# A copy of each tile's rows on GpSimd between the load and its readers, in a mixture-of-experts stage

## What is computed

```python
x = x + tanh(g_xattn[0]) * attention(layernorm(x), ctx, ctx, ...)      # 16 batches x 256 tokens x 256, 16 heads
x = x + tanh(g_ffn[0]) * ffn(layernorm(x), ...)
# ffn, E = 8 experts, K = 2 of them for each token:
bids = sigmoid(x @ conf_w.T + conf_b) * wealth
top_bids, selected = top_k(bids, 2)
combine = sum(one_hot(selected, 8) * softmax(top_bids)[..., None], axis=2)
expert_out[e] = (silu(x @ gate_w[e].T) * (x @ up_w[e].T)) @ down_w[e].T          # 256 -> 1024 -> 256
output = einsum('ebsh,bse->bsh', expert_out, combine)
```

## Time and profile before

| | |
|---|---|
| median of 3 runs | 1151.61 us (1150.68 to 1152.59) |
| the profiled execution | 1148.98 us |
| its span | 1147.2 us |
| TensorE busy | 1069.5 us, 93% |
| VectorE, ScalarE, GpSimd busy | 56%, 48%, 30% |
| mean granted TensorE clock | 0.971 |
| loads of `xg` | 39 of 272 KB |

### The profile page before, as it was taken

One profiled execution on the slowest core, in us unless ns is written; L12 is line 12 of the kernel. 1 busy time (PEld: TensorE's weight loads), 2 busy tenths in 40 slices (PEclk: granted clock), 3 DMA queues, 4 the chain that ended last, 5 costly groups with the idle time before them and its releaser, 6 DMA issues. The chain is left out here.

```text
span 1147.2 us, 24335 instructions
## 1 busy us (share of the span) xinstructions
PE 1069.5 (93%) x8310; PEld 892.5 (78%) x8310; DVE 647.4 (56%) x1575; ACT 547.4 (48%) x877; POOL 347.4 (30%) x404
## 2 busy tenths in 40 slices
PE   5789999999999978898999999999899999999994
PEld 4556767777777755575999999999579999999993
DVE  3657777777777764447444444444754444444442
ACT  4466777777777744445333333333643333333331
POOL 2024545554545552513112112112311211211211
PEclk8799999999999989999999999999999999999997
DMA  7000111111111173466212112112461211211211
GB/s 240 25 21 20 50 39 43 63 38 38 47 38 38 49 272 146 141 240 225 58 23 38 33 23 38 33 23 38 160 234 19 38 33 23 38 33 23 38 33 16
DMA packets 48426, 79.41 MB, mean 69 GB/s; under 512 B 6400, under 2 KB 42240, under 8 KB 44544
## 3 DMA queue, kind: packets, MB, share of 16 engines
q0 software_dynamic: 18080, 50.93, 16.5%
q1 hardware_dynamic: 30304, 27.95, 8.3%
HBM read 53.42 MB, written 25.18 MB: 69 GB/s over the span
## 5 line engine op out<-in xcount | busy, mean ns | idle before, releaser
L1809 POOL DMA_INDIRECT out<-y,token x64 | 103.7, 1620 | 473.3 <-DVE y L1693 352.7
L1585 ACT ACTIVATE silu<-gate 128x512 f32<-128x512 f32 x128 | 76.8, 600 | 277.0 <-PE up L1424 277.0
L960 DVE TENSOR_REDUCE max_neg<-maxps 128x4 f32<-128x1024 f32 x128 | 156.5, 1223 | 56.1 <-PE maxps L547 56.0
L1436 PE MATMUL down<-w_split,h_hi 128*128 128x512 f32 x512 | 185.8, 398 | 0.0
L1684 DVE TENSOR_TENSOR h<-silu,up 128x512 f32<-128x512 f32 x128 | 88.1, 688 | 171.0 <-ACT silu L1585 171.0
L1424 PE MATMUL gate<-x_hi,w_split 128*128 128x256 f32 x1024 | 184.1, 281 | 0.0
L1424 PE MATMUL up<-x_hi,w_split 128*128 128x256 f32 x1024 | 184.0, 281 | 0.0
L759 ACT ACTIVATE probs<-scores 128x1024 f32<-128x1024 f32 x124 | 127.3, 1026 | 86.4 <-PE scores L572 85.2
L1424 PEld LDWEIGHTS gate<-x_hi,w_split 128*128 128x128 f32 x1024 | 148.8, 188 | 2.9
L1424 PEld LDWEIGHTS up<-x_hi,w_split 128*128 128x128 f32 x1024 | 147.8, 188 | 0.0
L1438 PE MATMUL down<-w_split,h_lo 128*128 128x256 f32 x512 | 144.0, 281 | 0.0
(11 more groups left out here) (203 smaller groups left out, 1762.5 us busy)
## 6 DMA issues: line engine op xcount, KB each, us to landing
xg<-dispatched SPq DMA_DIRECT2D x39, 272.0 KB, 2.8
stage<-gate_T POOLq DMA_DIRECT2D x10, 1024.0 KB, 7.2
stage<-up_T POOLq DMA_DIRECT2D x10, 1024.0 KB, 9.4
stage<-down_T POOLq DMA_DIRECT2D x10, 1024.0 KB, 11.5
ctxT<-ctxT SPq DMA_DIRECT2D x17, 256.0 KB, 2.9
x_all<-x SPq DMA_DIRECT2D x16, 256.0 KB, 5.1
out<-x_all SPq DMA_DIRECT2D x16, 256.0 KB, 2.1
out<-y,token POOLq DMA_INDIRECT x70, 3.8
```

What stands on the lines that cost most here:

```text
L960: V.tensor_reduce(to, maxps[:], AX.X, ALU.max, negate=True).then_inc(s["max_taken"], 1)
L1436: mm(down[t][:].rearrange("p (n d) -> p n d", n=2), h_hi[:, i, rows], split[:, :, cols], start=i == 0, stop=False, skip_group_check=True)
L1585: nc.scalar.activation(silu[pair % 2][:], gate[pair % 2][:], ACT.Silu).then_inc(s_silu, 1)
L1809: pool.indirect_dma_start(out, bass.IndirectOffsetOnAxis(token[:, t:t + 1], axis=0), y[:, t, :], None, compute_op=ALU.add).then_inc(s_adde ...
```

## The change

A second buffer `rows` of the same shape as `xg`. GpSimd copies each landed tile from `xg` to `rows` (`copy_rows`), counted by the new semaphore `s_copied`. TensorE's transposes and VectorE's notes read `rows`. The load of the next tile waits for the copy and no longer for the notes. The copy of tile n+2 stands on GpSimd in body n, behind the (first) scatter, and waits until tile n+1 has been transposed and noted. VectorE's notes of tile n+1 move from the start of body n+1 into `next_rows` of body n, and take all eight weights of a row instead of one. Two unused loads run at the end instead of one. The two early tiles are still read from `xg`.

```diff
-        noted_weight = sb("noted_weight", [P, TT])
+        noted_weights = sb("noted_weights", [P, TT, EXPERTS])
+        rows = sb("rows", [P, TT, ROW])
...
             def first(e, r, n):
-                sp.wait_ge(s_noted, n)
+                if e == EARLY:
+                    sp.wait_ge(s_noted, EARLY)
+                else:
+                    sp.wait_ge(s_copied, n + (1 - EARLY) - 1)
...
             def rest(e, j, r, n):
-                sp.wait_ge(s_noted, n)
+                sp.wait_ge(s_copied, n + (1 - EARLY) - 1)
                 load_rows(j * TILE + (e * REGION + FIRST))
...
-            sp.wait_ge(s_noted, done + EXPERTS)
-            load_rows(0)
+            for more in range(2):
+                sp.wait_ge(s_copied, done + (EXPERTS + more - EARLY))
+                load_rows(0)
...
+            def turn_rows(copies):
+
+                pe.wait_ge(s_copied, copies)
+                turn(rows, 1)
...
-                turn_rows(n * 16 + 32)
+                turn_rows(n)
...
-            def note_rows(e):
-                V.tensor_copy(noted_token[:], xg[:, :, TOKCOL].bitcast(i32))
-                V.tensor_copy(noted_weight[:], xg[:, :, COMB + e]).then_inc(s_noted, 1)
-
-            def next_rows(r, n, firsts):
+            def note_rows():
+                V.tensor_copy(noted_token[:], rows[:, :, TOKCOL].bitcast(i32))
+                V.tensor_copy(noted_weights[:], rows[:, :, COMB:COMB + EXPERTS]).then_inc(s_noted, 1)
+
+            def next_rows(e, r, n, firsts):
...
                 V.tensor_copy(token[:], noted_token[:])
-                V.tensor_copy(weight[:], noted_weight[:]).then_inc(s_moved, 1)
+                V.tensor_copy(weight[:], noted_weights[:, :, e]).then_inc(s_moved, 1)
                 dve.wait_ge(s_moved, n + (1 - EARLY))
+                note_rows()
                 dve.wait_ge(s_down, n + 1)
...
+            def copy_rows(tile):
+
+                alone.wait_ge(s_rows, tile * 16 + 16)
+                if isinstance(tile, int) and tile == EARLY:
+                    pool.wait_ge(s_noted, EARLY)
+                else:
+                    pool.wait_ge(s_turned, tile)
+                    pool.wait_ge(s_noted, tile)
+                nc.gpsimd.tensor_copy(rows[:], xg[:]).then_inc(s_copied, 1)
...
             add_early(0, s_added)
             pool.wait_ge(s_added, 16)
+            copy_rows(EARLY)
             add_early(1, s_first_added)
             pool.wait_ge(s_down, EARLY)
             pool.wait_ge(s_rows, 16 * EARLY + 16)
             load_weights(EARLY + 1)
             attention_over(pool)
+            copy_rows(EARLY + 1)
...
                                         y[:, 0, :], None, compute_op=ALU.add).then_inc(s_first_added, 16)
+                copy_rows(n + 2)
...
                                             y[:, t, :], None, compute_op=ALU.add).then_inc(s_added, 16)
+                    if t == 0:
+                        copy_rows(n + 2)
```

More of the change, by code:

```diff
@@ L1283, in expert_stage @@
         s_xfull = sem("x_full_ready")
+        s_copied = sem("rows_copied")
         s_xhi = sem("x_hi_ready")
@@ L1406, in tensor_experts, with turn, turn_early_rows @@
             mm = nc.tensor.matmul
-            def turn_rows(after_load, tiles_turned=1):
-                pe.wait_ge(s_rows, after_load)
+            def turn(of, tiles_turned):
                 for t in range(TT):
                     for c in range(HC):
-                        last = nc.tensor.transpose(turned[:, c, t * P:(t + 1) * P], xg[:, t, c * P:(c + 1) * P], idn[:])
+                        last = nc.tensor.transpose(turned[:, c, t * P:(t + 1) * P], of[:, t, c * P:(c + 1) * P], idn[:])
                 last.then_inc(s_turned, tiles_turned)
+            def turn_early_rows():
+                pe.wait_ge(s_rows, 16 * EARLY)
+                turn(xg, EARLY)
+            def turn_rows(copies):
+                pe.wait_ge(s_copied, copies)
+                turn(rows, 1)
             def gate_up(pair, n):
@@ L1542, in tensor_experts @@
             pe.wait_ge(s["unit_read"], handed["units"])
-            turn_rows(16 * EARLY, EARLY)
+            turn_early_rows()
             turn_last_normed()
@@ L1572, in tensor_experts @@
             pe.wait_ge(s_flipped, 2 * EARLY)
-            turn_rows(16 * EARLY + 16)
+            turn_rows(1)
             over_tiles_hinted(pe, "pe_count", first, rest, before_rest)
@@ L1673, in next_rows @@
                 V.tensor_copy(token[:], noted_token[:])
-                V.tensor_copy(weight[:], noted_weight[:]).then_inc(s_moved, 1)
+                V.tensor_copy(weight[:], noted_weights[:, :, e]).then_inc(s_moved, 1)
                 dve.wait_ge(s_moved, n + (1 - EARLY))
+                note_rows()
                 dve.wait_ge(s_down, n + 1)
             def rest(e, j, r, n):
-                note_rows(e)
                 dve.wait_ge(s_flipped, 2 * firsts_by(e))
@@ L1687, in rest @@
                                     h_hi[:, 2 * pair:2 * pair + 2, :].bitcast(fp32), ALU.subtract).then_inc(s_hlo, 1)
-                next_rows(r, n, firsts_by(e))
+                next_rows(e, r, n, firsts_by(e))
                 for t in range(TT):
@@ L1723, in first @@
                 rest_of_weights(e, *HALVES[4:])
-                next_rows(r, n, e)
+                next_rows(e, r, n, e)
                 V.tensor_scalar(y[:, 0, :], down[0][:, 0:D], weight[:, 0:1], None, ALU.mult).then_inc(s_y, TT)
```

## The result

| | kernel before | changed kernel |
|---|---|---|
| median of 7 runs each, side by side | 1150.68 us (1147.77 to 1156.28) | 1143.32 us (1140.98 to 1148.32) |
| profiled execution, its span | 1148.98, 1147.2 us | 1148.32, 1146.6 us |
| ratio of the times | | 0.9932, 95% interval 0.9906 to 0.9958 |

The account below looks back on a forecast made before the run. TensorE, busy 93% of 1147.2 us, was taken as the bound, with 9.5 us of waits for the load of `xg`. Terms +1.5 - 0.8 - 3.7 - 1.5 + 0.3 = -4.2 us gave 1147.4 us, range 1143.8 to 1150.0.

Parts of the forecast that it names:

- the four waits: TensorE's transposes wait for the load of `xg`: before any body and in bodies 2, 5 and 22, 9.5 us together.
- body 2: First tile of expert 2: load issued ahead of the weights, so flip to last `contract` group shortens from 3.68 to 2.87, -0.8 us.
- body 5: First tile of expert 4: the 2.66 us wait and the half-clocked work behind it go, 6.59 against 2.87, -3.7 us.
- the price of a copy: A 128x544 float32 copy on GpSimd, taken by the element from a one-input cast: 0.65 us, 1.37 if dear.
- the loss at the transposes of tile 2: At the start, expert 2's first tile must be copied behind the first early scatter's landing, so TensorE starts 1.5 us later.
- copies cost nothing in rest bodies: Between a rest tile's two scatters GpSimd waits 3.03 us anyway, so a copy of 0.65 or 1.37 us costs nothing.
- the term of body 22: First tile of expert 6: GpSimd's copy waits for VectorE's pair of weight splits to end; -1.5 us, ends 0 and -4.2.
- an exchange of 0.25 us: In first bodies the note copies leave the start, ahead of the weight splits, for the end: counted as nothing.
- the +0.3 of body 21: First tile of expert 5: the copy ends at 816.5, TensorE wants it at 815.81; loss 0.3 us (0 to 0.8).
- the start: Before body 2: 1.5 us lost; if the clock comes back when it did before, half is not paid, 0.7 at least.
- Rival (a): In bodies 22 and 21 the copy slips in, never in the way: -7.2 to -8.0, 1143.6 to 1144.4 us; chance 0.20.

Follow-up runs that it names:

- three copies: Changed kernel with two more GpSimd copies of 128x512 float32 behind the copy of each rest tile, to an unread spare buffer; ratio 0.9978 to the kernel before.
- the second profile: Changed kernel run and profiled again with no edit; ratio 0.9942 to the kernel before, span 1141.7 us.
- notes moved: Kernel before, with the next tile's notes read out of `xg` at the end of the body before; no copy, no second buffer; ratio 0.9955.
- two one-buffer kernels with late weights: Kernel before, without and with its notes moved, second weight loads of experts 0 and 1 issued behind the scatters of bodies 22 and 23; ratios 0.9996 and 0.996.
- notes moved and late weights: Kernel before with notes moved and second weight loads of experts 0 and 1 issued later; no copy, one load buffer; ratio 0.996.

## Why the prediction was right and wrong

*Right, to 0.2 us:* the places of the four waits, the gain in body 2 (-0.8) and body 5 (-3.7), the price of a copy (0.64), the loss at the transposes of tile 2 (+1.34), and that copies cost nothing in rest bodies. The last stands the harder test of three copies.

*Wrong: the term of body 22.* "So I let the copy wait for the pair": forecast -1.5 us, measured -4.19. The step carried a scatter of 3.29 us over to a copy, and took VectorE's timetable from the kernel before. Both failed. Put among the splits on purpose, the copy waited for one of two and held the next; and the timetable had changed, since the moved notes shortened the scatters (2.02 us without any copy), with which VectorE's wait of 2.81 us went, so that the copy found 1.4 us without splits. Even in the old timetable the forecast had GpSimd free at 827.49, 0.12 us ahead of the pair, while the scatter that it went by had begun 0.49 us behind its pair; no run here tries the copy at that place in the old timetable. The forecast counted the moved notes as an exchange of 0.25 us, nothing. By the same step the +0.3 of body 21 was 0.

*Missed: what is late next.* Ahead of body 23 1.77 us were given back, behind the weights that GpSimd issues in body 22. The row was in the profile of before with 1.25 us, and I had no term for it. Without these weights the idle time is 1.0 us. So of 4.2 us won in body 22, TensorE kept 2.4. Why the idle time was 1.25 us before and 3.02 after, with the weights issued in the same place of the code, no run settles.

*Half missed: the start.* The loss of 1.34 us at the transposes was 0.70 at the first flip (0.92 in the second profile), the low end given for it.

With the measured terms the sum is +1.34 - 0.64 - 0.81 - 3.73 - 4.19 + 1.77 = -6.3 us. That is the difference of the profiles, and within the intervals of both timings (-7.8 and -6.7). Rival (a) was right about the copy, which was never in the way, and named -7.2 to -8.0; it was given 0.20. It had no term for the idle time ahead of body 23 either, so that its total agrees with the first timing is in part luck: by the profiles it is 0.9 us or more too much. The 1.5 us between -6.3 and -7.8 are within the interval, and nothing in the traces accounts for them. The range missed by 0.5 us, which is less than the 0.9 us by which the median of the kernel before lay lower in the second measurement than in the first. Still the forecast was half of what the timing gave, and two thirds to three quarters of what the profiles did.

## What to carry to other kernels

Before adding a buffer, ask what holds the one there is: here moving two small copies of 0.17 us to the end of the body before brought 5.2 of the 7 us (4.2 of some 6 by the profiles). A lead is worth what lies between issue and need, so the copy between load and reader paid here because the load moved a whole body ahead; with the load issued near the end of a body and not at its start, the kernel with this copy was 5 us slower than with neither. When a wait goes, look at the next idle time behind it, also at one put down to nothing: once the wait for the load was gone, moving six loads of weights by some ten microseconds took 2 us or more out of the idle time behind it and was worth 3 to 5 us, while in the kernel before the same edit brought nothing. That instructions fetched behind these weights are the cause was argued, not shown.

## What the runs showed of the hardware that I had not expected

- A GpSimd copy of 128x544 float32 beside a pair of VectorE operations with two SBUF inputs took 1.26 us including its wait, and lengthened the pair from 2.35 to 2.79 us. An indirect DMA from GpSimd at nearly the same place took 3.29 us when it began 0.49 us behind the pair's start and 2.01 when it began 0.62 behind.
- GpSimd's next operation starts 0.6 us before the record of an indirect DMA ends (826.21 against 826.82).
- Ahead of body 23, behind an empty loop, TensorE stood for 2.9 to 5.1 us in the two-buffer kernels with weights filling the DMA engines and no wait in body 22, for 1.2 us in the kernel before and with only the notes moved, where it had waited for the load in body 22, for 0.8 to 1.0 us in the two-buffer kernels without the weights, and not at all in the two one-buffer kernels with late weights.
- The length of an idle stretch alone does not tell what the clock does behind it. It stayed at its upper level behind 1.58 us (notes moved, body 5), 2.57 (notes moved and late weights, body 22), 3.02 and 3.06; it was granted at half behind 2.22 (notes moved, body 22), 2.66 (kernel before, body 5), 3.29 (for about 6 us), 3.41 and 5.09.
- The end of attention moved between 475 and 482 us (start of the first early contraction) in executions that do the same until then. A profiled time alone would have shown a gain of 0.7 us for this change.
